# The opening of a conditioned residual kernel: registers for addresses in place of gathers and one-hot products

## The reference

```python
x = x + einsum('bct,bcd->bdt', x, W0[subject])            # 200 matrices of 64 x 64
x = x + einsum('bct,bcd->bdt', x, W1[adapter])            # 8 matrices
x = x + einsum('bct,bcd->bdt', x, W2[adapter]) + bias[adapter][:, :, None]
gate = x @ Wg + (x @ Ag[adapter]) @ Bg[adapter]           # x as 64 rows of 512, to 2048
up   = x @ Wu + (x @ Au[adapter]) @ Bu[adapter]
h = silu(gate) * up
x = x + h @ Wd + (h @ Ad[adapter]) @ Bd[adapter]          # back to 512
```

## Time and profile before

| | us |
|---|---|
| median of 3 runs | 1235.41 (1234.34 to 1236.64) |
| the profiled execution | 1236.46 |
| its span, first to last instruction | 1234.4 |
| PE busy | 1223.5 |
| DVE busy | 962.9 |
| POOL busy | 742.1 |
| ACT busy | 568.8 |

### The profile page before, as it was taken

How to read it: one execution, slowest core, us unless ns; L and a number is a source line. 1 busy time by engine, 2 the same in 40 slices (tenths; PEclk the granted TensorE clock), 3 DMA queues, 4 the chain that set the end, 5 groups by cost and what they waited for, 6 DMA issues and landing times.

```text
span 1234.4 us, 18247 instructions
## 1 busy us (share of the span) xinstructions
PE 1223.5 (99%) x6214; PEld 1033.3 (84%) x6214; DVE 962.9 (78%) x1588; ACT 568.8 (46%) x1027; POOL 742.1 (60%) x622
## 2 busy tenths in 40 slices
PE   8999999999999999999999999999999999999998
PEld 7888888888888888888888888888888888888886
DVE  7987787887688787888678778778868877677775
ACT  3744455444544454554344544544534443444333
POOL 4577667648736667656864566675675554444453
PEclk9999999999999999999999999999999999999999
DMA  5866456456875355556496544546659442323423
GB/s 197 287 220 222 139 143 201 138 174 189 272 250 164 108 153 158 169 166 199 147 336 189 177 123 143 170 147 190 199 179 323 150 120 83 91 84 85 112 89 107
DMA packets 141690, 209.60 MB, mean 170 GB/s; under 512 B 44192, under 2 KB 88480, under 8 KB 141600
## 3 DMA queue, kind: packets, MB, share of 16 engines
q1 hardware_dynamic: 117696, 135.45, 35.3%
q0 software_dynamic: 23040, 71.85, 19.5%
q10 hardware_dynamic: 864, 1.15, 0.3%
HBM read 164.36 MB, written 44.04 MB: 169 GB/s over the span
## 4 chain that ended last, share of the span: by engine, by line
PE 95%; DVE 2%; issue 1%; POOL 0%; DMA 0%; another core or an unknown queue 0%; ACT 0%; DVEq 0%; POOLq 0%
PE pd L1770 29%; PE px L1770 28%; PE py L1770 14%; PE pz L1770 7%; PE pz L1787 3%; PE pv L1816 2%; PE pv L1814 2%; PE py L1787 2%; PE px L1787 2%; PE pd L1797 1%; PE px L1921 1%; PE py L1921 1%; PE pd L1906 1%; PE pd L1939 0%; PE pd L2076 0%
## 5 line engine op out<-in xcount | busy, mean ns | idle before, releaser
L813 POOL TENSOR_TENSOR h_lo<-g,h_hi 128x512 fp32r<-128x512 f32 x127 | 183.0, 1441 | 286.5 <-ACT h_hi L961 285.8
L776 POOL DMA_INDIRECT b_got<-b_table,idx_b x192 | 198.4, 1033 | 61.3 <-issue 52.4
L1770 PE MATMUL px<-xo_hi,wg_hi 128*128 128x512 f32 x516 | 207.3, 402 | 1.4 <-DVE wg_lo L1409 0.9
L1543 DVE TENSOR_TENSOR acc<-pd,acc 128x512 f32<-128x512 f32 x248 | 164.3, 684 | 51.3 <-PE pd L1770 50.0
L1770 PE MATMUL px<-xo_hi,wg_lo 128*128 128x512 f32 x516 | 202.5, 392 | 0.0
L1770 PE MATMUL px<-xo_lo,wg_hi 128*128 128x512 f32 x516 | 200.9, 389 | 0.0
L1409 DVE TENSOR_TENSOR wg_lo<-w_raw,wg_hi 128x512 fp32r<-128x512 f32 (+1 forms) x256 | 180.8, 712 | 25.9 <-ACT wg_hi L961 13.7
L1770 PE MATMUL pd<-wd_hi,h_hi 128*128 128x512 f32 x504 | 199.7, 396 | 0.0
L961 ACT ACTIVATE wg_hi<-w_raw 128x512 fp32r<-128x512 f32 (+1 forms) x260 | 146.0, 570 | 112.7 <-PE py L1787 55.1
L1770 PE MATMUL pd<-wd_lo,h_hi 128*128 128x512 f32 x504 | 197.9, 393 | 0.0
L1770 PE MATMUL pd<-wd_hi,h_lo 128*128 128x512 f32 x504 | 196.6, 390 | 0.0
(11 more groups left out here) (337 smaller groups left out, 2504.5 us busy)
## 6 DMA issues: line engine op xcount, KB each, us to landing
w_raw<-w_gu SPq DMA_DIRECT2D x65, 512.0 KB
wd_raw<-w_dn SPq DMA_DIRECT2D x64, 256.0 KB
xo_hi<-xops SPq DMA_DIRECT2D x21, 512.0 KB, 6.1
xo_lo<-xops SPq DMA_DIRECT2D x21, 512.0 KB, 7.1
acc<-x SPq DMA_DIRECT2D x8, 1024.0 KB, 8.8
ad_raw<-ad_table SPq DMA_DIRECT2D x16, 512.0 KB
ad_table<-ad_rows_kept SPq DMA_DIRECT2D x12, 512.0 KB
xops<-st_hi SPq DMA_DIRECT2D x24, 256.0 KB, 2.8
```

The source lines that it names most:

```text
L776: gp.indirect_dma_start(out=dst, out_offset=None, in_=rows_of, in_offset=bass.IndirectOffsetOnAxis(ap=rows.bitcast(U32), axis=0)).then_inc ...
L813: return gp.tensor_tensor(dst, src_raw, src_hi, ALU.subtract)
L1543: ins = dve.tensor_tensor(dst, pd[j][:, :], dst, ALU.add)
L1770: ins = pe.matmul(psum, w_parts[wi], x_parts[xi], start=(start and i == 0), stop=(stop and i == 2), skip_group_check=more)
```

## The change

It concerns only the opening. Numbers are read from memory into registers, by SP (the eight first samples of the pairs of quarter 0), ACT (the eight second ones) and PE (16 adapters). SP and ACT fetch each sample's rows of W0 by a transfer whose address holds the register, eight each. W0's, W1's and W2's matrices stand on 64 partitions, one sample or adapter beside the other, so that the table has eight matrices side by side, made by eight products in place of four (for 64 rows each). The one-hot matrices, the 32 products with them, the doubling and masking are gone: `o_combine` multiplies each sample's W0 part (the identity is already added, `first_sum`) with 64 columns of the table, whose place comes from the register, eight products for each half, and ACT copies the result, two pairs at a time. SP's first transfer is x of half 0, then the rows, x of half 1, and the weights of unit 0 and, after this x and `b`, of unit 1, with no wait for DVE. POOL asks for the adapter numbers, bias and subject numbers, makes the high part of the first weights and of `b`'s first piece (both were ACT's). DVE makes its row numbers, masks and selectors in other places; it waits for the adapter numbers ahead of the table's sum. On PE the layer products and turns are interleaved. The first warm-up has 2 calls in place of 14, the second 3 in place of 4.

```diff
-WARM_UP = (14, 4)
+WARM_UP = (2, 3)
+        def first_rows(engine, t, s, subjects):
+            of_half = w0_rows[s * SUBJECTS * C:(s + 1) * SUBJECTS * C].rearrange("(u c) n -> u c n", c=C)
+            for j in range(TP):
+                rows = of_half[bass.ds(subjects[j], 1)].rearrange("u c n -> (u c) n")
+                engine.dma_start(ea[t][:, 2 * j + s, :], rows).then_inc(oe_in[t], 16)
+        def first_values(engine, values, first, last, top):
+            _, loaded = nc.values_load_multi_w_load_instructions(
+                values.unsqueeze(0)[:, first:last], [engine], min_val=0, max_val=top - 1,
+                skip_runtime_bounds_check_because="inputs lie within the tables")
+            return loaded
...
-            sp.wait_ge(ints_in, 2 * 16)
-            sp.wait_ge(e0_in, 2 * 16)
             load_x(0, 0)
-            sp.wait_ge(pick_made, TP + 2)
-            load_weights(0)
-            sp.wait_ge(oe_in[0], TP * 16)
+            subjects = subjects_of(mybir.EngineType.SP, 0)
+            for t in range(2):
+                first_rows(sp, t, 0, subjects[t])
             load_x(0, 1)
+            load_weights(0)
             sp.wait_ge(x_in[0][1], 16)
             load_b(0)
+            load_weights(1)
             sp.wait_ge(oe_add, 1)
...
+            gp.dma_start(ints[:, 1, :], adapter.partition_broadcast(P)).then_inc(ints_in, 16)
+            gp.dma_start(bias_src, bias_pairs).then_inc(bias_in, 16)
+            gp.dma_start(ints[:, 0, :], subject.partition_broadcast(P)).then_inc(subjects_in, 16)
-            gp.wait_ge(idx_done, 1)
-            for t in range(2):
-                for j in range(TP):
-                    gather_rows(ea_four[t][:, j, :], w0_rows, idx_first[:, TP * t + j:TP * t + j + 1], oe_in[t])
+            gp.wait_ge(raw_in[0], 16)
+            for g in range(4):
+                gp.tensor_copy(wg_hi[:, 2 * g, :], w_raw[:, 0, g, :]).then_inc(w_hi_done[g], 1)
             gp.wait_ge(idx_a_done, 1)
             gather_ad(0, 0)
+            gp.wait_ge(*piece_in(0))
+            gp.tensor_copy(part(st_hi[:, piece(0)[0], :]), st_lo[:, piece(0)[0], :]).then_inc(b_hi_done, 1)
             b_low(0)
...
+            def first_sum(t):
+                dve.wait_ge(oe_in[t], 2 * TP * 16)
+                own_part = ea[t].rearrange("p (j s) (h n) -> p j (s h) n", s=2, h=2)[:, :, 0:4:3, :]
+                dve.tensor_tensor(own_part, own_part, ident[0:C, 0:C].unsqueeze(1).unsqueeze(1).to_broadcast([C, TP, 2, C]),
+                                  ALU.add).then_inc(ea_done, 1)
...
+            dve.tensor_tensor(es[:, :, C:2 * C], by_adapter(pv[0:C, :]), e2, ALU.add).then_inc(oe_add, 1)
+            first_sum(0)
+            row_numbers()
+            first_sum(1)
+            block_numbers()
+            tables()
+            gather_numbers()
+            selectors(0, 0)
...
+            adapters = first_values(mybir.EngineType.PE, adapter, 0, 2 * QP, ADAPTERS)
             pe.wait_ge(consts, 5)
             warm_up(WARM_UP[0])
...
             def o_combine(t):
-                pe.wait_ge(oe_in[t], TP * 16)
-                pe.wait_ge(eb_done, t + 1)
+                pe.wait_ge(ea_done, t + 1)
                 for j in range(TP):
-                    ins = pe.matmul((pv, py)[t][:, j * P:(j + 1) * P], ea_four[t][:, j, :], eb_four[t][:, j, :],
-                                    start=True, stop=True)
-                ins.then_inc(of_mm, 1)
+                    for s in range(2):
+                        first = j % 2 * P + s * C
+                        column = adapters[2 * (TP * t + j) + s] * (3 * C) + C
+                        ins = pe.matmul(of_banks[t][j // 2][:, first:first + C], ea[t][:, 2 * j + s, :],
+                                        es_cols[:, bass.ds(column, C)], start=True, stop=True)
+                    if j % 2:
+                        ins.then_inc(of_mm, 1)
...
+            o_combine(0)
+            o_layer(0)
+            o_layer(1)
             pe.wait_ge(bias_done, 1)
             o_combine(1)
             for j in range(TP):
+                o_layer(j + 2)
+                o_turned(0, j)
+            o_layer(6)
+            o_turned(1, 0)
+            o_layer(7)
+            for j in range(1, TP):
+                o_turned(1, j)
```

More of the change, by code:

```diff
@@ L224, in cond_resid_kernel @@
+        f_four = [four(up0[:, :]), four(vacc[:, 0, :])]
+        bias_src = vacc[:, 1, 0:P]
         eq_row = st_a21[:, 2 * C:2 * C + PAIRS]
         r_seq = st_a21[:, 2 * C + PAIRS:2 * C + PAIRS + QS].bitcast(I32)
[L226 to L230, removed]
+        of_banks = ((pz, pd[2]), (px, pv))
@@ L231, in cond_resid_kernel, with subjects_of @@
+        def subjects_of(engine, s):
+            loaded = first_values(engine, first_subjects, s * QP, (s + 1) * QP, SUBJECTS)
+            return loaded[:TP], loaded[TP:]
         a2_raw = [acc[:, 1, i:i + 2, :].rearrange("p a n -> p (a n)") for i in (0, 6)]
@@ new lines, in _, with o_a1_high @@
+                for i in range(2):
+                    act.wait_ge(of_mm, 2 * t + i + 1)
+                    copy(f_four[t][:, 2 * i:2 * i + 2, :], four(of_banks[t][i][:, :])[:, 0:2, :]).then_inc(of_kept, 1)
+            def o_a1_high(j):
+                act.wait_ge(o_turn, j + 1)
+                copy(xo_hi[:, A11:A12 + 1:2, :].rearrange("p k (c n) -> p k c n", c=2)[:, :, :, j * P:(j + 1) * P],
+                     pd[j][:, :].rearrange("p (k c n) -> p k c n", k=2, c=2)).then_inc(o_a1_hi, 1)
@@ L1025, in keep_s1 @@
+            o_bias(2)
+            for j in range(TP):
+                o_a1_high(j)
+                o_bias(j + 3)
+            o_bias(QP - 1)
+            for j in range(TP):
+                act.wait_ge(o_turn, TP + j + 1)
+                copy(acc[:, 1, :, j * P:(j + 1) * P].rearrange("p (k c) n -> p k c n", c=2)[:, 0:4:3],
+                     turn_banks[j][:, :].rearrange("p (k c n) -> p k c n", k=2, c=2)).then_inc(o_a2_kept, 1)
             def keep_s1(n):
@@ L1453, in _ @@
-            for j in range(TP):
-                ins = dve.tensor_scalar(eq_first[:, j, :], adf[:, 0:2 * QP], p_f[:, 4:5], float(2 * j),
-                                        ALU.subtract, ALU.is_equal)
-            link(ins)
-            picks(0)
+            dve.tensor_tensor(e2, w2_all, ident[0:C, 0:C].unsqueeze(1).to_broadcast([C, ADAPTERS, C]), ALU.add).then_inc(e2_done, 1)
+            dve.wait_ge(ints_in, 16)
+            for s in range(2):
+                rows = slice(s * C, (s + 1) * C)
+                dve.tensor_copy(pair_ad[rows, :], ints[rows, 1, :].rearrange("p (q s) -> p q s", s=2)[:, :, s])
@@ L1458, in _ @@
+            link(dve.tensor_copy(adf, ints[:, 1, :]))
+            dve.tensor_scalar(eq_row, pair_ad[:, :], p_f[:, 1:2], None, ALU.is_equal).then_inc(eq_done, 1)
             dve.wait_ge(e2_done, 1)
             dve.wait_ge(oe_mm, 1)
-            dve.tensor_tensor(es_four[:, :, C:2 * C], four(pv[:, 0:TP * C]), e2_four, ALU.add).then_inc(oe_add, 1)
-            for p in range(1, TP + 2):
-                picks(p)
-            picked(0)
-            for p in range(TP + 2, QP):
-                picks(p)
@@ L1486, in _ @@
             ins.then_inc(o_a1_done, 1)
-            selectors(0, 0)
             sums(1)
+            dve.wait_ge(e_out, 2 * 16)
             for i in range(2):
@@ L1946, in _ @@
             pe.wait_ge(e2_done, 1)
-            for j in range(TP):
-                ins = pe.matmul(pv[:, j * C:(j + 1) * C], w1_four[:, j, :], e2_four[:, j, :], start=True, stop=True)
+            for i in range(ADAPTERS):
+                ins = pe.matmul(pv[0:C, i * C:(i + 1) * C], w1_all[:, i, :], e2[:, i, :], start=True, stop=True)
             ins.then_inc(oe_mm, 1)
```

167 lines of the change are left out of this document (49 added, 118 removed).

## The result

The changed kernel takes 1236.89 us at the median of 20 runs (1235.73 to 1241.58), the kernel before 1234.82 (1234.09 to 1236.64): a ratio of 1.0027, 95% interval 1.0019 to 1.0034. It is slower by 0.27%, where 1231.9 was forecast, and it lies above the range (1228.3 to 1235.3). The median hides something: 12 of the 20 runs lie between 1235.73 and 1236.99 and the other 8 between 1240.36 and 1241.58, with nothing between and the same granted clock on record. The profiled execution, 1235.97 us with a span of 1233.8, is one of the lower group.

A forecast was written before the change was run, and what follows sets the result against it. PE bounds the kernel, so only the opening counts: 10.3 + 14.04 + 1.2 + 1.3 + 0.3 = 27.1 us for 30.65, 3.5 earlier; 1235.41 - 3.5 = 1231.9 us, range 1228.3 to 1235.3.

The forecast's parts named there:

- the split: Start of PE's first split product, the end of the opening: forecast at 27.1 us for 30.65, 3.5 us earlier.
- follower: Work needed after PE's earlier start (x (0, 1), weights, b tables): claimed to move earlier by more than PE does.
- The amount of PE work: PE from its start to the first split product: 11.39 us as before plus 2.65 for more combining calls, 14.04 us.
- fewer warm-ups: PE's opening with warm-up calls cut: the half-pace loss falls mostly on the path, 0 to 1.4 us, taken 1.3.
- turns at half pace: Sign of a wrong forecast: PE's turns in the opening running at half pace.
- SP's queue in front of the weights: Slower rival: one read and eight register-addressed transfers delay x (0, 1) and weights; 1243 at 2.5 us a transfer; chance 0.06.
- The start: When the first combining products can start on PE, where table and rows paths meet: taken 10.3 us (9.3 to 12.5).
- The table path: Landing of w1 and w2 at 6.2 us, then addition, products, sums and handovers up to the first combining: 10.35 us.
- the rows path: SP's register reads (3.7 us), four row transfers at 0.45 each, landing 2.7 us later, then the sum: 10.05 us.
- register operands: PE's sequencer working out columns for 16 combining calls: 0 to 4.8 us, a quarter taken, 1.2 us.
- given back on the path: Rival: register operands at 0.30 us each or issues at 1.25; split products start at 30.4 to 30.7, 1235.2; chance 0.19.
- DVE stall counted as gone: Unexplained 2.3 us before DVE's addition to the first combining products; gone because ACT copies instead, not expected elsewhere.

The follow-up runs named there:

- the second trace of before: The unchanged kernel before, run and profiled once more: 1234.96 us, span 1232.9.
- the best kernel: Changed kernel with x of half 0 behind all eight SP row transfers, PE's reads in two parts, first-half turns later, warm-ups 12 and 12: 1232.70 us, ratio 0.9964.
- the changed kernel's second trace: The changed kernel run again unaltered in the fifth set: median 1236.61 us, ratio 1.0014; its profiled execution took 1240.59 us.

## Why the prediction was wrong

**What was right.** All is decided in the opening, and the time follows the split one to one: split and span are 26.62 and 1229.5, 28.21 and 1231.1, 30.66 and 1233.8, 35.49 and 1238.5, 38.76 and 1241.3, a distance of 1202.5 to 1203.1 each (the largest of any run was the 1204.2 of 26.13 and 1230.3). In the changed kernel no follower (x (0, 1), weights, b tables) became a bound. The amount of PE work, 14.04 us, was right as well: from the first combining to the split the lower group took 30.66 - 12.93 = 17.73, and 14.04 + 3.05 (pace, below) + 0.30 (registers) leaves 0.34, for 0.3 taken for handovers.

**The step that failed most: "fewer warm-ups", 1.3 us, 0 to 1.4.** I read the ramp off the first 3 us of the old warm-ups and took it for the whole price. In the changed kernel the combining lost 3.61 - 1.92 = 1.69 and the first two layer products 3.27 - 1.91 = 1.36 (1.91 is their time behind 14 warm-ups), 3.05 in all, beside the table product's 0.8 and the slow warm-ups ahead of the start. In the upper group, 15 of its 35 runs, a further 4.4 was lost in the one trace of it. The whole error of the lower group's split, 30.66 for 27.1, is 3.5: 2.6 from the start (0.8 of it this same pace), 1.75 from this term, less 0.9 for the registers. In the upper group the pace is most of it. I had even named turns at half pace as a sign of being wrong, but had given them no price and no chance. The kernel with only this line changed, at 9 us, is the direct measure, and the row for the ramp stood there: rows 9 show that the ramp ran under cover. I didn't ask how long it lasts once the cover is gone. Beyond the 1.4 there should have been a rival, and it would have been the slower one; mine, SP's queue in front of the weights, did not occur (0.65 us a transfer, weights out at 11.3).

**The start, 10.3 forecast, 12.93 measured.** Three terms were small. The table path had `w1` in at 6.2; it was in at 7.8, because it now flies with x (behind small transfers it lands in 2.6 us instead of 6.3). On the rows path SP's reads took 4.2 for at most 3.7, and the transfers 0.65 each for 0.45; this path didn't set the start, since DVE begins its first sum of rows at 11.71 without a wait for them. And PE's own sixteen reads, left out of the sum as lying beside the landing, held PE until 7.9 without a warm-up and so fed the first error. After them PE never waits until the combining: 1.19 + 1.90 + 0.56 + 1.44, at half pace, are the 5.1 us from 7.91 to 13.00. With x behind the small transfers the same 16 reads end at 4.71, eight of SP's in 2.1. The Trainium skill (Runtime: NRT & Kernel Launch, Instruction fetch mechanics) gives 200 ns a register; 2.1 / 8 is 0.26 here with little else in flight and 4.2 / 8 is 0.52 behind x, so its figure is near the first and far below the second.

**The term that was too large: register operands, 1.2 us, 0 to 4.8.** Eight calls with register columns take 1.03 + 0.89 = 1.92 us at full pace, 0.15 over the 1.77 forecast for plain ones, and with constant columns they take no less at either pace. Sixteen cost at most 0.3. The rival built on it (given back on the path) had about the right end for the lower group, 30.4, for the wrong reason: that is luck.

**The baseline.** Most of the 2.3 us of DVE stall counted as gone was missing from the second trace of before, whose split is at 29.50. If that is the usual run, the median was to be set against 29.50, and 1.15 of my 3.5 us never existed. From 29.50 the lower group loses 1.2 us, the upper 6.0; the medians of the groups (1236.4 and 1241.0) lie 1.6 and 6.1 above 1234.82, which fits.

**What is left open.** The split of the start's loss between PE's silence and the landing of `w1` isn't exact, since both end at 8 us: taking the reads away alone moved the table product by 0.6 us, and keeping PE warm without them the split by 4.5 (30.66 to 26.13). What decides in a run whether the half pace ends at 20 or at 29 us was not found, nor what decides whether an idle behind the warm-ups brings it back.

## What to carry to other kernels

Warm-ups that lie under a wait cost nothing and look useless in a profile. Before cutting them, putting a register read ahead of them, or leaving an idle behind them, price the first dense stage at half pace for its full length. Read numbers into registers and issue the small transfers that others wait for before the first large load, all of them and not half; with the load between the reads and the transfers that use them, the reads were quick and the transfers late. Register-addressed operands and row transfers cost here what the same ones with constant numbers did.

## What the runs showed of the hardware

- Register reads took longer with a large load in flight: eight on SP 2.1 us, or 4.2 behind a 1 MB load; sixteen on PE were over at 4.71 or at 7.9 us. PE did nothing meanwhile. Small transfers issued beside that load land in 4.6 to 6.7 us, with SP's reads ahead of it the bias and the subject numbers in up to 9.0, instead of 2.5 to 3.8.
- In four traces PE idled after a full warm-up (1.54, 2.21, 1.45 and 1.74 us), and the granted clock went to 0.50 during or after that idle and stayed there for 10.2, 6.8, 3.4 and 13.7 us. In a fifth an idle of 1.89 us was followed by full pace. Three kernels whose traces have at most 0.34 us of idle there (14 and 4 warm-ups, with x first and with x behind the rows, and the best kernel) have all their runs in one group, 1.1 to 1.7 us wide; a fourth with 0.34 us (the reads in two parts, x first) spread over 6.4 us all the same.
- DVE's subtraction of low parts (128x256) was held up in some traces while POOL's on 128x1024 ran beside it. In the changed kernel's second trace the four took 4.43 us. In its first, where this subtraction of POOL began at 23.83, after them, they took 1.42:

```profile
21.40 4.43 DVE L1471 TENSOR_TENSOR wg_lo<-w_raw,wg_hi 128x256 fp32r<-128x256 f32 x4
22.80 2.41 POOL L817 TENSOR_TENSOR st_lo<-st_lo,st_hi 128x1024 fp32r<-128x1024 f32 x1
```

This reached the split in one trace only, that of the reads in two parts with x first (0.85 us). No experiment separated the two engines, so this is an observation only.
